# First layer of a two-layer kernel: softmax weights and row mixing moved up, and the second batch's tiles finished without lag

## What is computed

```python
f = rfft(xn); corr = irfft(f * conj(f))            # autocorrelation of each row
weights, delay = top_k(corr, 6)                    # int(log(512)) = 6
w = softmax(weights)
s = sum_j w[j] * roll(xn, -delay[j])               # six shifted copies of each row, mixed

logits = xn @ gate_w                               # sum of the two largest of 8
h = relu(xn @ up_w) ** 2                           # 512 x 1024
y = h @ down_w + ((xn @ fc1) @ expert) * (sum of two largest logits) @ fc2
g = silu(layernorm(y, gamma, beta))
x = x + s * g                                      # goes to layer 2
```

## Time and profile before

| | us |
|---|---|
| median of 3 runs | 2144.74 |
| lowest, highest | 2140.62, 2145.65 |
| the profiled execution, device time | 2139.39 |
| its span in the trace | 2137.4 |
| first layer, from the start of the span to the start of layer 2's first instruction | about 255 |
| mean granted TensorE clock over the span | 0.976 |

### The profile page before, as it was taken

The page is one execution under the profiler, slowest core; times in us unless marked ns, Lnnn a source line. Parts: engine busy times, 40 slices in busy tenths (PEclk is TensorE's granted clock), DMA queues, the critical chain, the costliest instruction groups (busy, mean ns, idle before and its releaser), DMA issues.

```text
span 2137.4 us, 36923 instructions
## 1 busy us (share of the span) xinstructions
PE 2013.5 (94%) x10994; PEld 1606.0 (75%) x10994; DVE 1574.1 (74%) x2963; ACT 1468.1 (69%) x2931; POOL 1197.2 (56%) x823
## 2 busy tenths in 40 slices
PE   6989578998899999999999999999999999999986
PEld 5556256666688888888878888888888888888875
DVE  4353758885677777777777877877777878787777
ACT  3131465553677777878877877877787878787774
POOL 2323255664365656665656666665665665655655
PEclk9999789999999999999999999999999999999999
DMA  7212322334332333333333333232333333332333
GB/s 272 81 58 73 110 70 79 124 102 139 118 121 93 134 102 124 107 130 112 113 112 114 109 113 124 100 132 92 126 127 107 113 125 111 113 117 94 129 119 119
DMA packets 113840, 243.51 MB, mean 114 GB/s; under 512 B 23648, under 2 KB 24672, under 8 KB 112736
## 3 DMA queue, kind: packets, MB, share of 16 engines
q1 hardware_dynamic: 109792, 228.37, 31.8%
q0 software_dynamic: 3840, 12.59, 1.9%
HBM read 228.06 MB, written 12.85 MB: 113 GB/s over the span
## 4 chain that ended last, share of the span: by engine, by line
PE 70%; DVE 3%; issue 2%; ACT 1%; DVEq 0%; ACTq 0%
PE s_ps L71 12%; PE s_ps L73 12%; PE s_ps L72 12%; PE s_ps L1505 6%; PE s_ps_o L71 5%; PE s_ps_o L73 5%; PE s_ps_o L72 5%; PE s_ps L1475 5%; PE s_ps L1513 4%; PE s_ps L1467 3%; PE s_ps L1495 1%; PE s_ps L1453 1%; DVE xs L1775 1%; DVE s_state L1707 0%; DVE s_hdt L1719 0%
## 5 line engine op out<-in xcount | busy, mean ns | idle before, releaser
L1887 POOL TENSOR_TENSOR w_lo<-w_raw,w_hi 128x1024 fp32r<-128x1024 f32 x142 | 340.1, 2400 | 558.5 <-ACT w_hi L1567 558.5
L71 PE MATMUL s_ps<-h_hi,w_hi 128*128 128x512 f32 x1152 | 463.1, 402 | 9.2 <-DVE s_hid L1736 6.1
L73 PE MATMUL s_ps<-h_hi,w_lo 128*128 128x512 f32 x1152 | 450.7, 391 | 0.0
L72 PE MATMUL s_ps<-h_lo,w_hi 128*128 128x512 f32 x1152 | 449.5, 390 | 0.0
L1731 DVE SCALAR_TENSOR_TENSOR s_cv<-s_ps,s_par,s_cv 128x511 f32<-128x511 f32 (+2 forms) x480 | 355.8, 744 | 18.4 <-ACT s_cv L1610 12.6
L1904 POOL TENSOR_TENSOR s_lm<-s_lm,s_cbt 128x512 f32<-128x512 f32 x256 | 326.1, 1297 | 12.5 <-ACT s_lm L1592 12.5
L1585 ACT ACTIVATE s_lm<-s_rows,s_steps 128x128 f32<-128x128 f32 x1024 | 312.5, 390 | 2.0 <-PE s_ps L1505 2.0
L1610 ACT ACTIVATE s_cv<-s_ps,s_par 128x512 f32<-128x512 f32 x160 | 124.7, 779 | 235.9 <-PE s_ps L73 219.7
L71 PEld LDWEIGHTS s_ps<-h_hi,w_hi 128*128 128x128 f32 x1152 | 217.1, 188 | 54.4 <-DVE s_hid L1736 6.9
L73 PEld LDWEIGHTS s_ps<-h_hi,w_lo 128*128 128x128 f32 x1152 | 216.8, 188 | 47.0
L72 PEld LDWEIGHTS s_ps<-h_lo,w_hi 128*128 128x128 f32 x1152 | 217.7, 189 | 40.9
(11 more groups left out here) (232 smaller groups left out, 4131.5 us busy)
## 6 DMA issues: line engine op xcount, KB each, us to landing
w_raw<-in_w_in SPq DMA_DIRECT2D x144, 512.0 KB, 3.2
s_rows<-acs_dram SPq DMA_DIRECT2D x256, 256.0 KB, 4.3
s_wo_raw<-in_w_out SPq DMA_DIRECT2D x128, 256.0 KB, 3.5
w_raw<-in_gu_q SPq DMA_DIRECT2D x14, 512.0 KB, 3.2
f_d_q<-in_d_q SPq DMA_DIRECT2D x28, 256.0 KB, 2.6
f_d_w<-in_d_s SPq DMA_DIRECT2D x28, 256.0 KB, 3.5
table<-xn SPq DMA_DIRECT2D x16, 256.0 KB, 8.7
xs<-in_x SPq DMA_DIRECT2D x8, 256.0 KB, 4.3
```

The lines of the kernel that those rows point to most:

```text
L71: nc.tensor.matmul(dst, l_hi, r_hi, start=start, stop=False)
L72: nc.tensor.matmul(dst, l_hi, r_lo, start=False, stop=False)
L73: return nc.tensor.matmul(dst, l_lo, r_hi, start=False, stop=stop)
L1887: nc.gpsimd.tensor_tensor(w_lo[:, slot, :], w_raw[:, slot, :], w_hi[:, slot, :].bitcast(F32), ALU.subtract).then_inc(w_lo_ready, 1)
```

## The change

Three things are altered, all of them orders of instructions; no arithmetic and no DMA is added or taken out.

1. ScalarE takes the exponentials of a batch right after the eight up-projection evictions, ahead of the `a_lat` and `a_exo` evictions.
2. VectorE mixes tiles 0 and 1 right after the correlations, ahead of the logits, and tiles 2 and 3 right behind the logits. (A wait for the split of `fc1w` is added before the very first mix, since `mixed` shares its memory.)
3. The finishing loop has `lag = 1 - n`: the first batch keeps its stagger, in the second batch each tile is finished in one step: rout, square root, Silu on ScalarE, and add, norm, multiply on VectorE.

```diff
@@ scalar, in the loop over n
                     nc.scalar.activation(hid[:, m, :], ps_a[:, i % 4, :], ACT.Relu).then_inc(act_took, 1)
+                for t in range(TB):
+                    g = n * TB + t
+
+                    act.wait_ge(topk_ready, g + 1)
+                    nc.scalar.activation(wexp[:, g, 0:TOPK], top[:, g, 0:TOPK], ACT.Exp, bias=negmax[:, g:g + 1],
+                                         accum_out=wsum[:, g:g + 1]).then_inc(weights_ready, 1)
                 for m in range(KL):
                     i = a_lat(n, m)
...
-                for t in range(TB):
-                    g = n * TB + t
-
-                    act.wait_ge(topk_ready, g + 1)
-                    nc.scalar.activation(wexp[:, g, 0:TOPK], top[:, g, 0:TOPK], ACT.Exp, bias=negmax[:, g:g + 1],
-                                         accum_out=wsum[:, g:g + 1]).then_inc(weights_ready, 1)
-                for t in range(TB + 2):
+                lag = 1 - n
+                for t in range(TB + 2 * lag):
...
-                    if t >= 2:
-                        act.wait_ge(affine_ready, g - 1)
-                        nc.scalar.activation(z[:, t - 2, :], z[:, t - 2, :], ACT.Silu).then_inc(silu_ready, 1)
-                    if 1 <= t <= TB:
-                        act.wait_ge(zvar_ready, g)
-                        nc.scalar.activation(zstd[:, g - 1:g], zmv[:, g - 1, 1:2], ACT.Sqrt).then_inc(zstd_ready, 1)
+                    if lag:
+                        act_silu(n, t - 2)
+                    act_std(n, t - lag)
+                    if not lag:
+                        act_silu(n, t)
@@ vector
+            def mix(n, t):
+                g = n * TB + t
+                dve.wait_ge(weights_ready, g + 1)
+                link(nc.vector.reciprocal(wrec[:, g:g + 1], wsum[:, g:g + 1]))
+                link(nc.vector.tensor_scalar(wexp[:, g, 0:TOPK], wexp[:, g, 0:TOPK], wrec[:, g:g + 1], None,
+                                             ALU.mult))
+                if g == 0:
+                    dve.wait_ge(dft_split, 3)
+                dve.wait_ge(gathered[g % 2], 16 * TOPK * (g // 2 + 1))
...
                     nc.vector.tensor_scalar(negmax[:, g:g + 1], top[:, g, 0:1], -1.0, None,
                                             ALU.mult).then_inc(topk_ready, 1)
+                mix(n, 0)
+                mix(n, 1)
                 for t in range(TB):
                     g, i = n * TB + t, d_log(n, t)
                     dve.wait_ge(pe_d, i + 1)
...
-                for t in range(TB):
-                    g = n * TB + t
-                    dve.wait_ge(weights_ready, g + 1)
...
-                for t in range(TB + 2):
+                mix(n, 2)
+                mix(n, 3)
+
+                lag = 1 - n
+                for t in range(TB + 2 * lag):
...
-                    if 1 <= t <= TB:
-                        u = g - 1
+                    if 0 <= t - lag < TB:
+                        u = g - lag
...
-                    if t >= 2:
-                        u = g - 2
+                    if t >= 2 * lag:
+                        u = g - 2 * lag
```

More of the change, by code:

```diff
@@ L299, in _, with act_std, act_silu @@
         def _(act):
+            def act_std(n, t):
+                if 0 <= t < TB:
+                    g = n * TB + t
+                    act.wait_ge(zvar_ready, g + 1)
+                    nc.scalar.activation(zstd[:, g:g + 1], zmv[:, g, 1:2], ACT.Sqrt).then_inc(zstd_ready, 1)
+            def act_silu(n, t):
+                if 0 <= t < TB:
+                    act.wait_ge(affine_ready, n * TB + t + 1)
+                    nc.scalar.activation(z[:, t, :], z[:, t, :], ACT.Silu).then_inc(silu_ready, 1)
             act.wait_ge(var_ready, NT)
@@ L393, in _ @@
                                         ALU.subtract).then_inc(up_lo_ready, 1)
+            def mix(n, t):
+                g = n * TB + t
+                dve.wait_ge(weights_ready, g + 1)
[5 more added lines that the diff above has]
+                dve.wait_ge(gathered[g % 2], 16 * TOPK * (g // 2 + 1))
+                link(nc.vector.tensor_scalar(mixed[:, t, :], shifted[:, g % 2, 0, :], wexp[:, g, 0:1], None, ALU.mult))
+                for j in range(1, TOPK):
+                    add = nc.vector.scalar_tensor_tensor(mixed[:, t, :], shifted[:, g % 2, j, :], wexp[:, g, j:j + 1],
+                                                         mixed[:, t, :], ALU.mult, ALU.add)
+                    if j < TOPK - 1:
+                        link(add)
+                add.then_inc(mixed_ready, 1)
             dve.wait_ge(rows_loaded, 48)
@@ L440, in _ @@
                                                 ALU.add).then_inc(zvar_ready, 1)
-                    if 1 <= t <= TB:
-                        u = g - 1
+                    if 0 <= t - lag < TB:
+                        u = g - lag
                         dve.wait_ge(zstd_ready, u + 1)
                         link(nc.vector.reciprocal(zrstd[:, u:u + 1], zstd[:, u:u + 1]))
-                        link(nc.vector.scalar_tensor_tensor(z[:, t - 1, :], z[:, t - 1, :], zmv[:, u, 0:1], gamma[:],
+                        link(nc.vector.scalar_tensor_tensor(z[:, t - lag, :], z[:, t - lag, :], zmv[:, u, 0:1], gamma[:],
                                                             ALU.subtract, ALU.mult))
-                        nc.vector.scalar_tensor_tensor(z[:, t - 1, :], z[:, t - 1, :], zrstd[:, u:u + 1], beta[:],
+                        nc.vector.scalar_tensor_tensor(z[:, t - lag, :], z[:, t - lag, :], zrstd[:, u:u + 1], beta[:],
                                                        ALU.mult, ALU.add).then_inc(affine_ready, 1)
-                    if t >= 2:
-                        u = g - 2
+                    if t >= 2 * lag:
+                        u = g - 2 * lag
                         dve.wait_ge(silu_ready, u + 1)
                         dve.wait_ge(mixed_ready, u + 1)
-                        link(nc.vector.tensor_tensor(mixed[:, t - 2, :], mixed[:, t - 2, :], z[:, t - 2, :], ALU.mult))
-                        nc.vector.tensor_tensor(x1[:, u, :], x1[:, u, :], mixed[:, t - 2, :],
+                        link(nc.vector.tensor_tensor(mixed[:, u % TB, :], mixed[:, u % TB, :], z[:, u % TB, :], ALU.mult))
+                        nc.vector.tensor_tensor(x1[:, u, :], x1[:, u, :], mixed[:, u % TB, :],
                                                 ALU.add).then_inc(x1_ready, 1)
```

## The result

The changed kernel takes 2149.64 us (median of 9 runs, 2144.72 to 2153.13), the kernel before 2143.51 beside it (9 runs, 2140.62 to 2145.65): ratio 1.0031, 95% interval 1.0021 to 1.0042. The forecast was 2123.6, with a range of 2117 to 2130: wrong in size and in sign, by 26 us. The loss itself is small, 0.3%. The span of the profiled execution is 2147.6 us; forecast was 2116.3.

The account below looks back on a forecast made before the run. TensorE, busy 94%, was taken to lose time waiting 5.8 us at the batch boundary and 23.1 us at layer 2's start, and at lower clock. Gains 8.6 + 12.5 = 21.1 us: 2144.74 to 2123.6 us, range 2117 to 2130.

Parts of the forecast that it names:

- Exponentials moved up: ScalarE's exponentials ahead of the `a_lat` eviction: ending by 76.0, before that eviction at 76.29, delaying nothing; cost nothing.
- Mixing moved up: VectorE's mixes, first batch: mix 0 starts at 76.4, mix 3 ends at 103.2 to 105 instead of 121.96.
- Both are covered: Slowed fetch issues beside mixing make mix 3 end at 105 and mix 1 0.6 us later, without delaying TensorE.
- the 2.3 us of cover for `d_shared`: Tile 0's `d_shared` starts at 90.97 and its bank is free by 88.7, so later logits have 2.3 us to spare.
- First batch's finish: Batch boundary: first square at 136.0 against 141.51, gaining 5.5 us, plus 3.1 us from the clock not falling: 8.6 us.
- Second batch's finish: End of layer 1: tiles finished one by one, 7.7 us each, end 242.2 against 254.69: gain 12.5 us.
- the 1.38 us on top that made a rival: ScalarE table loads cost drain beyond 1.28 us and stand out in the finishing loops; 2133.9 us, chance 0.02.
- Sum: Whole kernel: 8.6 + 12.5 = 21.1 us gained, median 2123.6 us.
- Slower than before: Fetched rows land late, logits wait, TensorE stalls at tile 0's `d_shared`; 15.8 us per batch, 2155 us; chance 0.02.

Follow-up runs that it names:

- both_lag: The changed kernel with the stagger kept in the second batch too; 2128.60 us (0.9922), and 2160.76 us (1.0071) when repeated unchanged in a later series.
- half_rows: The changed kernel with only the first half of each row fetched (1 KB instead of 2 KB), as many fetches; 2120.93 us, ratio 0.9889.
- series 4: Fourth set of follow-up kernels, run one after the other on one chip beside the kernel before (median 2144.1 us there).
- lag_only: The kernel before with only the second batch finished tile by tile without lag, exponentials and mixing where they were; 2146.87 us, ratio 1.0000.
- hold_short: The changed kernel with GpSimd's fetches for tiles 2 and 3 held until the logits are taken and mix 1 moved behind the logits; 2129.59 us, 0.9926.
- mix_behind: The changed kernel with all four mixes of a batch behind the logits on VectorE; 2132.20 us, ratio 0.9928.
- light_mix: The changed kernel with four of the five multiply-adds of each mix left out; 2155.82 us, ratio 1.0041.
- logits_first: The changed kernel with the logit matmuls and their top-8 moved ahead of the correlations; 2130.72 us, ratio 0.9929.
- pe_waits_60: The changed kernel with 60 already fulfilled waits ahead of TensorE's first transpose; 2130.84 us, ratio 0.9939.

## Why the prediction was wrong, step by step

**Exponentials moved up: right.** They run at 63 to 74 us; the first `a_lat` eviction follows at 74.49, where it was.

**Mixing moved up: right in its times, wrong in "Both are covered".** Mix 0 starts at 74.42, which is 76.2 in the old trace's times (forecast 76.4), with two slowed issues beside mix 0 (1.14 and 1.27 us) and three beside mix 1 (1.04, 1.27 and 1.27). The step that failed is the 2.3 us of cover for `d_shared` (1.7 with the 0.6 us that I gave mix 1 myself). Without the stall the step holds: both_lag takes its first logit at 88.69. I priced what fetches and mixing do to one another and took it that TensorE's logits would be ready by 88.7 whatever ran beside them. They were taken at 93.9 to 98.7. In the sum this is a term that I put at nothing. Counted from the first top-8 of one batch to that of the next, half_rows (no stall) takes 161.66 - 62.65 = 99.0 us and the changed kernel 174.70 - 61.50 = 113.2: the stall costs 14.2 us there. From the second batch's first top-8 to layer 2's first matmul (L939, at 234.47 and 263.44) it is 72.8 against 88.7: 15.9 us. Together 30.1 us, against a gain of 22.5. Layer 2's first matmul in the kernel before, the changed kernel and half_rows:

```profile
257.58 1.97 PE L920 MATMUL m_ps<-ident,xs 128*128 128x128 f32 x8 [23.07 <-DVE xs L1039]
...
263.44 1.97 PE L939 MATMUL m_ps<-ident,xs 128*128 128x128 f32 x8 [10.63 <-DVE xs L1058]
...
234.47 1.97 PE L939 MATMUL m_ps<-ident,xs 128*128 128x128 f32 x8 [10.63 <-DVE xs L1058]
```

These prices set half_rows of series 4 beside the changed kernel of its own series; both fetch as often, half_rows half the bytes.

**What the trace of before could show, and what not.** Its twelfth fetch is issued at 80.03 and GpSimd then waits for a mix, so its fetches pause early in the logits (78.8 to 84.7). The change removes this pause. I counted it as time to be won; lag_only and hold_short show that it also bounds the stall. But the trace itself gave no warning: rows land beside the logits up to about 84, and TensorE keeps its pace all the same:

```profile
78.80:84.50 5.70, 5.70 (x49) 5.69 (x47) 1.00 (x6) 0.60 (x1) 1.88 (x2) 0.92 0.49 147
```

That TensorE itself might slow down once logits and fetches overlap to the end was in none of my bounds.

**First batch's finish: right.** Without the stall the batch takes 99.0 us against 170.71 - 63.30 = 107.4 before: 8.4 us less, forecast 8.6. In the changed kernel itself TensorE waits 0.37 us at the boundary (forecast 0.4), and the granted clock after it is 1.00, TensorE's upper level, not 0.51:

```profile
148.50:154.80 6.30, 5.93 (x27) 4.75 (x26) 3.81 (x7) 2.56 (x6) 1.03 (x1) 1.00 0.22 83
```

**Second batch's finish: right.** The four tiles are finished one by one, the last routed product is taken at 252.84 and VectorE ends at 260.55, 7.7 us later as worked out. A table load takes 1.28 us and the next instruction starts at its end (139.88 behind the load of 138.59, 141.83 behind that of 140.53): the 1.38 us on top that made a rival did not show. half_rows gains 14.1 us in this part against 12.5; 1.4 of it could be that the last logit of the second batch was already that much late in the kernel before (22.9 us after the first top-8, against 21.5 in mix_behind).

**Sum.** half_rows starts layer 2 at 234.47 against 257.58 before: 23.1 us, forecast 21.1 (0.6 of it is an earlier start of the first batch in its trace). Its 2120.9 us lie 2.7 under the forecast. That the changed kernel would take about this time in a series without the stall is argued from there, not shown: it ran in two series, both with it.

**The rivals.** "Slower than before" had the right place and almost the right price: `d_shared` stalls, 12.7 + 3.1 us per batch, 2155 us; measured were 14.2 and 15.9 us. That the price fits is luck, for it was worked out from fetches at 2.5 us each. The cause was wrong, rows that land late, and from that cause's rarity came its chance of 0.02. The rows landed on time; TensorE itself was late. A rival should have been priced by what waits at the place, whatever the cause. The Trainium skill's rule on the ports shared by VectorE and GpSimd ("SBUF — State Buffer", "SBUF: two separate sides") does not account for the stall either: light_mix stalls with VectorE idle for 15 us.

**Behind layer 1.** From layer 2's first matmul to the end the changed kernel needs 1884.2 us, the kernel before 1879.8: a further 4.4 us. This is mostly a matter of which execution was profiled. The kernel before was profiled in one 4.1 us under its median, the changed kernel in one at its median. The medians differ by 6.1 us, and 5.9 of these are the later start of layer 2. The same program differs as much between two executions: the changed kernel needs 1884.2 and 1886.7 us behind layer 1, both_lag 1883.0 and 1886.9.

**What stays open.** By which mechanism fetches in flight slow TensorE to one instruction per 0.7 or 1.4 us, why it begins in the changed kernel at about 77 us, where the logits begin, although the fetches run from 64, and what makes it come and go between series. Whether ordinary transfers would do the same if they ran without a pause from ahead of the logits is not tested. What the runs show is this: in a series that has the stall, it begins while GpSimd's fetches are in flight, lasts as long as they do and ends when they pause.

## What to carry to other kernels

Before removing a wait, list what ran apart because of it, on every engine, and give the new overlap a price that is not only that of the two parts you move. Where many row fetches from GpSimd are in flight beside TensorE's work, let them pause: here one wait for GpSimd (and mix 1 moved behind the logits) bounded the delay of the logits to about 3 us per batch, where the stall cost about 15. Moving the small matmuls out of the way of the fetches (logits_first) is untested in a series with the stall. And repeat a surprising result, unchanged, in another series before explaining it: the theories here rested on runs that differed in their series as well as in their edits.

## What the runs showed of the hardware

**One program, two times.** both_lag took 2125.5 to 2131.0 us in one series and 2151.8 to 2162.2 in another, each series consistent within itself. The kernel before moved by only 3.4 us between series (medians 2143.5 to 2146.9). Its fetches pause, which may be why; it was profiled once only.

**Sixty waits at the start, and 13 us more behind the first layer.** pe_waits_60 starts layer 2 at 233.65, 0.8 us ahead of half_rows in the same series, but needs 1897.7 us from there, against 1884.4. The profiled execution is the slowest of its three, 2.5 us over their median; still, no other profile here needs more than 1886.9. TensorE's waits in it from 600 to 2100 us, then those of half_rows (line numbers are one less there):

```profile
PEld s_ps L1525 <- issue: 10.7, 11, 1.8
```

```profile
PEld s_ps L1524 <- issue: 2.3, 7, 0.4
```

One of TensorE's six gaps of over 1 us before L1525, in order of time, and the DMA queues from 1058.2 to 1059.2 (packets, MB, share):

```profile
1058.31 0.87 PE L1525 MATMUL s_ps<-s_lm,s_hdt 128*64 128x128 f32 x11
1060.78 0.54 PE L1525 MATMUL s_ps<-s_lm,s_hdt 128*64 128x128 f32 x5 [1.60 <-issue]
```

```profile
q8 instruction: 1, 0.02, 6.7%
```

The gap stands where 16 KB of instructions are fetched in the middle of a run of short matmuls. All six gaps have such a fetch close by, between 2.2 us before their start and 0.3 behind it, and the trace has only 104 fetches in its 2131 us, one in 20 us; most of them leave no gap. The waits shift where in the program they fall. That this makes all of the 13 us is not shown: the waits above account for 8.4. The Trainium skill ("Runtime: NRT & Kernel Launch", "Instruction fetch mechanics") calls the cost of such a crossing mostly hidden. That agrees with the rest of this trace, but not with short matmuls, where one crossing shows up to 1.6 us here and 1.8 in the changed kernel (before L1532, at 883.35).
